# Attention's output product from tile 6 on: one fp32 product becomes three products of rounded upper and lower parts

## What is computed

```
out = einsum('bhqk,bhkd->bhqd', softmax(q k^T / 4), v)        # 16 heads, 64 keys
x   = x + einsum('bse,fe->bsf', out, Wo) + bo                  # Wo: 256 x 256, the product that changes
x   = x + shared(layernorm(x)) + top-2-of-8 experts(layernorm(x))
```

## Time and profile before

| | us |
|---|---|
| median of 3 runs | 330.73 (329.1 to 345.86) |
| the profiled execution, time | 330.43 |
| the profiled execution, span of the core | 328.7 |
| PE busy | 310.7, 95% of the span |
| DVE busy | 229.1, 70% |
| ACT busy | 216.4, 66% |
| POOL busy | 187.8, 57% |

### The profile page before, as it was taken

One profiled execution on the slowest core, in us unless ns is written; L12 is line 12 of the kernel. 1 busy time (PEld: TensorE's weight loads), 2 busy tenths in 40 slices (PEclk: granted clock), 3 DMA queues, 4 the chain that ended last, 5 costly groups with the idle time before them and its releaser, 6 DMA issues.

```text
span 328.7 us, 7700 instructions
## 1 busy us (share of the span) xinstructions
PE 310.7 (95%) x2402; PEld 272.4 (83%) x2402; DVE 229.1 (70%) x474; ACT 216.4 (66%) x438; POOL 187.8 (57%) x228
## 2 busy tenths in 40 slices
PE   8999999999999999989999996999999999999980
PEld 7767767767788889978998885999999999999980
DVE  0899999889775478597674653657687767666630
ACT  1566688777967968736665535667698678678540
POOL 5558989788950076776460036324364558556654
PEclk9999999999999999999999997999999999999995
DMA  7980000062101932357626482444455467445243
GB/s 235 401 338 11 1 2 1 2 214 91 34 1 39 344 124 91 114 172 202 237 100 178 95 263 62 67 86 78 72 88 86 68 99 107 70 51 64 35 53 45
DMA packets 27911, 36.34 MB, mean 111 GB/s; under 512 B 8384, under 2 KB 22336, under 8 KB 27488
## 3 DMA queue, kind: packets, MB, share of 16 engines
q1 hardware_dynamic: 20128, 25.42, 25.1%
q0 software_dynamic: 7456, 10.04, 17.8%
q10 hardware_dynamic: 288, 0.39, 0.4%
HBM read 22.64 MB, written 13.19 MB: 109 GB/s over the span
## 4 chain that ended last, share of the span: by engine, by line
PE 46%; POOL 16%; DVE 12%; issue 11%; DMA 7%; SPq 4%; ACT 3%; ACTq 0%; POOLq 0%; DVEq 0%
PE psS L1316 13%; POOL xg_d L447 10%; PE psP L1332 7%; PE psP L1336 4%; DVE mx L918 4%; DMA xg_d<-rows_b,slots 3%; PE psP L1387 2%; PE psS L1363 2%; DMA s_free<-in_b 2%; POOL Pr L477 2%; DVE Pr L927 2%; PE psP L1263 2%; PE psD L1231 2%; POOL s_free L507 1%; PE psS L1111 1%
## 5 line engine op out<-in xcount | busy, mean ns | idle before, releaser
L516 POOL DMA_INDIRECT out<-xres,meta x39 | 64.6, 1658 | 37.8 <-DMA out<-xres,meta 22.0
L912 DVE TENSOR_TENSOR h_lo<-g,h_hi 128x512 fp32r<-128x512 f32 x32 | 25.3, 791 | 27.9 <-ACT g L612 27.8
L611 ACT ACTIVATE h_hi<-psS,sb1T 128x512 fp32r<-128x512 f32 x32 | 22.1, 690 | 30.3 <-PE psS L1208 29.2
L477 POOL TENSOR_TENSOR Pr<-Pr,inv 128x1024 f32<-128x1024 f32 x16 | 31.3, 1957 | 11.3 <-DVE inv L949 11.2
L742 ACT ACTIVATE s_hi<-psS,b1c 128x256 fp32r<-128x256 f32 x60 | 25.5, 487 | 14.5 <-PE psS L1316 14.5
L1332 PE MATMUL psP<-w_lo,s_hi 128*128 x120 | 29.8, 282 | 0.0
L1332 PE MATMUL psP<-w_hi,s_hi 128*128 x120 | 29.7, 280 | 0.0
L1055 DVE TENSOR_TENSOR s_lo<-sraw,s_hi 128x512 fp32r<-128x512 f32 x30 | 20.6, 687 | 12.4 <-ACT sraw L745 12.4
L1208 PE MATMUL psS<-xt_hi,s_lo 128*128 128x512 f32 x64 | 25.9, 404 | 0.0
L745 ACT ACTIVATE sraw<-psS,b1c 128x256 f32<-128x256 f32 x60 | 25.8, 500 | 0.0
L1208 PE MATMUL psS<-xt_lo,s_hi 128*128 128x512 f32 x64 | 25.2, 394 | 0.0
(11 more groups left out here) (249 smaller groups left out, 1011.3 us busy)
## 6 DMA issues: line engine op xcount, KB each, us to landing
wraw<-in_w SPq DMA_DIRECT2D x16, 512.0 KB, 6.0
xg<-xg_d SPq DMA_DIRECT2D x15, 256.0 KB, 2.7
xres<-in_x SPq DMA_DIRECT2D x4, 512.0 KB, 7.5
sraw<-in_sw SPq DMA_DIRECT2D x2, 1024.0 KB, 12.3
out<-xres SPq DMA_DIRECT2D x4, 512.0 KB
xTs<-in_xT SPq DMA_DIRECT2D x3, 512.0 KB, 8.8
xg<-xg_d SPq DMA_DIRECT2D x9, 128.0 KB, 2.0
xg_d<-filler SPq DMA_DIRECT2D x8, 130.0 KB, 2.0
```

Of the source, the lines that this page charges most:

```text
L477: pool.tensor_tensor(out=Pr[:, t % NPR], in0=Pr[:, t % NPR], in1=inv[:, t % 2].unsqueeze(2).to_broadcast([P, NH, L]), op=ALU.mult).then_in ...
L516: pool.indirect_dma_start(out, bass.IndirectOffsetOnAxis(ap=meta[:, n, 0:1].bitcast(U32), axis=0), y[:, n % NYB], None, compute_op=ALU.add ...
L611: A.activation(h_hi[:, n % 2], h_bank[n % 2], ACT.Gelu, bias=bias).then_inc(hhi_done, 1)
L912: V.tensor_tensor(out=h_lo[:, n % 2], in0=g[:, n % 2], in1=h_hi[:, n % 2].bitcast(F32), op=ALU.subtract).then_inc(hlo_done, 1)
```

## The change

From tile 6 on (`SPLIT_O = 6`) ACT copies `psA` to an fp32r upper part, DVE subtracts it from `psA` for a lower part at the end of its iteration s (tile s-3), and PE runs six fp32r products per tile instead of two fp32 ones. ACT makes the upper part of `WoT` once in iteration 6 and DVE the lower part once in iteration 8. PE's transposes of rows (L1220) overwrite half of the same bank and now wait for the lower part too. The four new buffers lie in `xt_hi[:, 1]` and `xt_lo[:, 1]`, which `x_high(1)` fills later. Cut to its core:

```diff
+SPLIT_O = 6
+        Wo_hi, Wo_lo = [xt_hi[:, 1, i].rearrange("p (c n) -> p c n", c=C) for i in range(2)]
+        OT_hi, OT_lo = [xt_lo[:, 1, i].rearrange("p (b c n) -> p b c n", b=2, c=C) for i in range(2)]
# ACT
+                if q == 1:
+                    act.wait_ge(att_psum, NT)
-                    A.activation(OT[:, t % 2], psA[:, D:2 * D].rearrange("p (c n) -> p c n", c=C), ACT.Copy).then_inc(ot_sb, 1)
+                    A.activation(OT[:, t % 2] if t < SPLIT_O else OT_hi[:, t % 2], psA[:, D:2 * D].rearrange("p (c n) -> p c n", c=C), ACT.Copy).then_inc(ot_sb, 1)
+                if s == SPLIT_O:
+                    act.wait_ge(ld_wo, 16)
+                    A.activation(Wo_hi, WoT[:], ACT.Copy).then_inc(wohi_done, 1)
# DVE, between the reciprocal (L949) and x_low(0)
+                if s == SPLIT_O + 2:
+                    dve.wait_ge(wohi_done, 1)
+                    V.tensor_tensor(out=Wo_lo, in0=WoT[:], in1=Wo_hi.bitcast(F32), op=ALU.subtract).then_inc(wolo_done, 1)
+                if SPLIT_O <= s - 3 < NT:
+                    t = s - 3
+                    dve.wait_ge(ot_sb, t + 1)
+                    dve.wait_ge(att_psum, t - 1)
+                    V.tensor_tensor(out=OT_lo[:, t % 2], in0=psA[:, D:2 * D].rearrange("p (c n) -> p c n", c=C),
+                                    in1=OT_hi[:, t % 2].bitcast(F32), op=ALU.subtract).then_inc(otlo_done, 1)
# PE, before the transposes L1220
+                    if min(s - 3, NT) > SPLIT_O:
+                        pe.wait_ge(otlo_done, min(s - 3, NT) - SPLIT_O)
# PE, the product
-                    for c in range(C):
-                        last = T.matmul(psD[:, 0:D], OT[:, t % 2, c], WoT[:, c], start=(c == 0), stop=(c == C - 1))
+                    if t < SPLIT_O:
+                        for c in range(C):
+                            last = T.matmul(psD[:, 0:D], OT[:, t % 2, c], WoT[:, c], start=(c == 0), stop=(c == C - 1))
+                    else:
+                        pe.wait_ge(otlo_done, t - SPLIT_O + 1)
+                        pe.wait_ge(wolo_done, 1)
+                        i = 0
+                        for c in range(C):
+                            for a, b in ((OT_hi, Wo_lo), (OT_hi, Wo_hi), (OT_lo, Wo_hi)):
+                                last = T.matmul(psD[:, 0:D], a[:, t % 2, c], b[:, c], start=(i == 0), stop=(i == 3 * C - 1))
+                                i += 1
```

More of the change, by code:

```diff
@@ L187, in program @@
         sum_done, inv_done, probs_done = sem("sum_done"), sem("inv_done"), sem("probs_done")
-        pt_psum, pt_sb, ot_psum, ot_sb, att_psum = sem("pt_psum"), sem("pt_sb"), sem("ot_psum"), sem("ot_sb"), sem("att_psum")
+        pt_psum, pt_sb, ot_psum, ot_sb, otlo_done, att_psum = sem("pt_psum"), sem("pt_sb"), sem("ot_psum"), sem("ot_sb"), sem("otlo_done"), sem("att_psum")
+        wohi_done, wolo_done = sem("wohi_done"), sem("wolo_done")
         xbo_done, x1_done, sbh_done = sem("xbo_done"), sem("x1_done"), sem("sbh_done")
```

## The result

The changed kernel took a median of 336.45 us (334.23 to 337.67, six runs), the kernel before 329.92 beside it (328.27 to 345.86): a ratio of 1.0198, with a 95% interval of 1.016 to 1.0236. It is slower by some 2%, and whether by more or less than 2% is open; 336.0 had been forecast. A later measurement, on another chip, gave 335.50 against 328.55, a ratio of 1.0216 (1.0177 to 1.0255). Some executions are slower by a few per cent whatever the kernel; the medians include them and the ratios do not, so a ratio need not be the quotient of the two medians beside it.

The account below looks back on a forecast made before the run. The chain of waits, alternating mainly between DVE and PE up to the first scatter, was taken as the bound. Terms 0.5 + 1.0 + 1.7 + 1.4 + 1.1 - 0.45 = +5.3 us gave 336.0 us, range 332.0 to 339.5.

Parts of the forecast that it names:

- Where the path runs, and that the first scatter hands everything on: Chain of waits alternates mainly between DVE and PE; whatever moves the first scatter moves the end by as much.
- `Wo_lo`, +0.5: Iteration 8, DVE against POOL: POOL's scaling and PE's transposes behind it come later, +0.5 us, bounds 0.5 and 2.3.
- Products of tiles 6 to 8, taken as 0: Six fp32r products between fp32 work on PE: price per tile between -0.15 and +0.04 us, taken as 0.
- `OT_lo`, three times +0.34: Lower parts of tiles 9, 10 and 11 lengthen the DVE stretch in iterations 12 to 14, +1.0 us.
- `x_low(0)`, +1.7: Iteration 13 on DVE: `OT_lo` pushes it behind POOL's L477, so it stands until that ends, +1.7 us, bounds 0 and 1.9.
- The order on PE, +1.4: Ahead of L1220, PE's queue waits for `OT_lo`: 3.4 us in place of 2.0 between reciprocal and 87.27, +1.4 us.
- The wait of 4.7 us in iteration 15 and the lower clock, +1.1: PE stands 4.7 us for DVE, then runs at a lower clock: 1.7 us lost less 0.6 slack, +1.1 us.
- Tiles 13, 14 and 15: Their products lie in the PE stretch behind 87.27 and save 0.15 us each, -0.45 us.
- the long loss of `Wo_lo`: Rival: POOL takes the 51.43 slot and yields only after L477 or later; 337.8 or 341 us, chance 0.2.
- nor did PE count: Rival: all ten products save 0.15 us on PE, lower parts hide in DVE's waits; 329.2 us, chance 0.05.
- `x_low(0)` was blocked: Rival denied this: not blocked by POOL, PE's wait 3.1 us, sum +2.5 us; 333.2 us, chance 0.15.
- the lower clock came in every profile of the change: Rival denied this: no lower clock, all else as forecast, sum 4.2 us; 334.9 us, chance 0.15.

Follow-up runs that it names:

- no_wo_low: Changed kernel with DVE not making `Wo_lo`, the first product using `Wo_hi` twice: 331.86 us beside 328.64 for the kernel before, ratio 1.0103.
- hidden_first: Changed kernel with `shared_hidden` ahead of the transposes that wait for `OT_lo`, iterations 15 to 17: 332.40 us beside 328.64 for the kernel before, ratio 1.0105.
- transposes_repeated: Changed kernel with PE's transposes of the probabilities in iteration 14 run four times over: 333.40 us beside 328.55 for the kernel before, ratio 1.0173.
- after_third: Changed kernel measured again, nothing edited, on another chip: 335.50 us beside 328.55 for the kernel before, ratio 1.0216.
- second and third group: Two of three groups of follow-up runs, each group on one chip beside the kernel before, which took 328.64 and 328.55 us there.
- split_13: Changed kernel with three products for tiles 13 to 15 only and `Wo_lo` in iteration 16: 329.15 us beside 328.64 for the kernel before, ratio 1.0034.
- products_only: Changed kernel without `OT_lo` and PE's wait for it, `(OT_hi, Wo_hi)` added twice: 331.09 us beside 335.16 for the kernel before, ratio 0.9976.
- both_orders: Changed kernel with `shared_hidden` ahead of PE's waiting transposes and `x_low(0)` ahead of `OT_lo`: 331.55 us beside 328.64 for the kernel before, ratio 1.0103.
- after: The changed kernel itself, in its first profile: median 336.45 us beside 329.92 for the kernel before, ratio 1.0198.
- after_again: Changed kernel measured again with more rounds, nothing edited: 341.33 us beside 335.16 for the kernel before, ratio 1.0373.
- pe_kept_busy: Changed kernel with five unused matmuls on PE during its wait in iteration 15: 338.43 us beside 335.16 for the kernel before, ratio 1.0119.
- x_low_first: Changed kernel with `x_low(0)` moved back ahead of `OT_lo` of tile 10: 335.85 us beside 335.16 for the kernel before, ratio 1.0143.

## Why the prediction was right, point by point

- *Where the path runs, and that the first scatter hands everything on*: right. +5.02 at the scatter, +5.08 at the end.
- *`Wo_lo`, +0.5*: the mechanism was right (DVE wins, POOL's L473 waits in its stead, PE's stretch opens later), 0.40 by the start of the transposes and 0.38 by `no_wo_low`. But most of it was made good within the same stretch, by a term that had been put at nothing:
- *Products of tiles 6 to 8, taken as 0*: here the forecast was wrong. The 0.19 us that the first fp32r matmul seemed to cost in the earlier trace rows is no price of a change of format: six products between fp32 work take 0.71 us, all included. Tiles 6 and 8 gain 0.15 each (0.40 to 0.24 to 0.09); in tile 7's iteration PE waits 0.17 us for a copy of ACT (L625) and gains nothing. Together +0.1 at DVE's stretch instead of +0.5.
- *`OT_lo`, three times +0.34*: 0.33, 0.28 and 0.33 by the distance of the rows around them (0.28 where `x_low(0)` follows), 0.94 in place of 1.0. Right.
- *`x_low(0)`, +1.7*: 2.87 us against 1.18, and undone by moving it. Right, shown.
- *The order on PE, +1.4*: right. With the clock at full speed 4.18 us are left at iteration 16, and 4.18 - 0.1 - 0.94 - 1.69 = 1.45. It is what the other terms leave over, and `hidden_first` takes it and the clock's share away by an order on PE alone.
- *The wait of 4.7 us in iteration 15 and the lower clock, +1.1*: 4.69 us, and 1.1 us by `transposes_repeated` (109.04 against 110.16 at the scatter). Right in this execution; in another it was 0.5 more. Both ends of the wait stood 0.4 earlier than forecast, since the 0.5 of `Wo_lo` was in both, so its length came out. That the lower clock comes after waits of half this length too (2.38 us, and 1.90 behind 1.23) had not been foreseen, and makes shortening the wait a weaker cure than it looks.
- *Tiles 13 to 15, -0.45*: 0.28 between iteration 16 and the scatter, in the change and in `transposes_repeated` alike. Some 0.15, one product, too much, and it is tile 14's: from PE's L1240 of one iteration to the next the change is 0.14 shorter in iterations 17 (4.20 against 4.34) and 19 (3.76 against 3.90), and equal in iteration 18 (6.24).

Sum of what was measured: 0.1 + 0.9 + 1.7 + 1.45 + 1.1 - 0.3 = 5.0, forecast 5.3. The medians, however, lie 6.5 and 7.0 apart, and the two profiled executions only 3.8 (334.23 against 330.43). The forecast was set against the profiled execution of the kernel before, whose first scores began at 10.19, where the thirteen other profiles have 8.8 to 9.8; nothing in the change reaches that far forward, so this is taken to be chance. These 1.4 us are what lies between the path's 5.1 and the 3.7 of the two spans, and a start that is usually earlier fits the medians of 328.55 and 328.64 that the kernel before has elsewhere. The profiled execution of the change, in turn, is the fastest of its six, 2.2 under their median, with a mean clock of 0.979 where the other five have 0.970 to 0.975: they had more of the lower clock than this profile shows. `after_third` (0.974) shows 0.5 of it in iteration 15. From the scatter to the end the kernels with the whole sum in the second and third group need 211.4 to 214.5 us, so the tail adds a spread of its own. How much of the 6.5 each of these makes up is argued, not shown. So the 5.3 of the forecast is near the 5.0 of the path by its terms, and 336.0 near 336.45 partly by luck: the path was sized 0.3 too long, the start was set 1.4 too late, and the 2.2 us by which the median of the change lies above its profile were in no term.

Of the rivals, the long loss of `Wo_lo` did not happen (0.63 us at 49.97), nor did PE count: of the 1.5 us that ten products save on PE, 0.6 (tiles 6, 8, 13 and 15) are seen on the path, and they are outweighed. `x_low(0)` was blocked, and the lower clock came in every profile of the change.

By the Trainium skill, "SBUF — State Buffer", section "Who interferes with whom", the instruction that issues first holds the port. L798 and L481 agree with it on either side of the swap, with 0.16 us of lead and 0.11 of lag, and so does L961 with its lead of 0.10. `hidden_low(0)` does not, see below.

## What to carry to other kernels

Work taken off the busiest engine pays only where that engine is on the chain of waits; here the engine that does the preparing (DVE) was the chain, and a producer put on it makes the busiest engine wait with its whole queue behind it. When an operation is put between a producer and a two-input operation in SBUF, look at what the other engine of the port will start in the meantime: 0.34 us inserted cost 1.7 beside it. And an idle stretch of PE of 2 us and more may have to be charged twice, with its length and with the clock behind it; before taking it away, see which small waits it covers.

## What the runs showed of the hardware

**A DVE instruction that starts ahead of POOL's and stands all the same.** The forecast read 89.12 in the earlier trace rows as a lead of 0.05 us that was too short. That reading is wrong: in `split_13` L922 begins 0.51 us ahead of POOL's L482 and still stands through it and L445, 4.21 us where 0.69 are normal. In all three cases where it began ahead of POOL's L477 (or its like) and lost (4.21 us there, 3.78 in `products_only`, 3.76 before) POOL was issuing an ordinary DMA when DVE's instruction began. Before:

```profile
88.52 0.62 POOL L429 DMA_DIRECT2D out<-filler  x1
```

Beside an indirect one it is not so: in the change the same instruction begins during the first scatter (118.97 to 120.24) and takes its normal time:

```profile
119.19 0.68 DVE L921 TENSOR_TENSOR h_lo<-g,h_hi 128x512 fp32r<-128x512 f32 x1
```

But there no POOL instruction on SBUF followed. Whether the plain DMA's issue holds DVE back until POOL's next instruction comes, or something that goes along with it does, no run has separated; it stays open.

**A waiting DVE is sometimes let in between POOL's L481 and L444, and sometimes not.** In before, `products_only`, `hidden_first`, `both_orders`, `transposes_repeated` and `split_13` it stands to the end of the second (2.40 us and more). In the change it is let in: L481 runs from 91.48 to 93.38, DVE's instruction takes 0.78 us, and POOL's second one pays with 1.73 instead of 1.29:

```profile
93.15 0.78 DVE L921 TENSOR_TENSOR h_lo<-g,h_hi 128x512 fp32r<-128x512 f32 x1 [0.73 <-ACT g L618]
```

```profile
93.35 1.73 POOL L444 TENSOR_TENSOR s_lo<-sraw,s_hi 128x512 fp32r<-128x512 f32 x1
```

There DVE came 0.23 us before L481 ended, and in the six others 0.60 us (`transposes_repeated`) or more. An equal subtraction (L1043) is served among the eight L507 at 194.63 before, with 1.22 us for a normal 0.69. Whether it is the time left to POOL's first instruction that decides was not tested.

**When the clock falls, and for how long.** In seven of the profiles the clock fell to 0.50 around iteration 15. PE had then been idle, or had begun again, as follows (us from the start of the span, to 0.1):

| kernel | PE's last idle stretch | clock at 0.50 |
|---|---|---|
| `after` | 77.6 to 82.3 | 82.8 to 86.2 |
| `after_again` | 77.9 to 82.6 | 82.7 to 86.1 |
| `after_third` | 77.9 to 82.6 | 80.5 to 87.3 |
| `no_wo_low` | 77.6 to 82.3 | 80.7 to 87.5 |
| `pe_kept_busy` | 77.6 to 80.0 | 79.9 to 83.3 |
| `hidden_first` | 78.5 to 80.9 | 81.7 to 85.1 |
| `x_low_first` | 79.8 to 81.7, and 1.23 before | 82.0 to 85.4 |

So the first four kernels, with the same wait of 4.7 us, were given the lower clock up to 2 us before work set in again or up to 0.5 after it, and 3.4 us of it or 6.8; and after 2.38 us of idleness the first work ran at 0.50 in one kernel and at 1.00 in another. A wait of 2.06 us (`transposes_repeated`) and waits of 1.23 and twice 0.5 (`both_orders`) left the clock at 1.00.
